# Prologue of a fused cross-attention and expert-FFN kernel: another order of work on five engines

## What is computed

```
x = x + xattn(layernorm(x), ctx)
x = x + ffn(layernorm(x))

xattn:  q, k, v = projections (16 heads of 8);  scores = q k^T / sqrt(8)
        out = softmax(scores v) over the 8 features of a head;  heads @ wo^T + bo
ffn:    t = rmsnorm(x) * norm_w;  2 of 8 experts by softmax(t @ gate^T)
        h1 = t w1^T + 2 (t a1^T) b1^T per expert;  h3 likewise
        act = silu(h1) * h3;  out_e = act w2^T + 2 (act a2^T) b2^T
        out = sum over the two experts, weighted
```

## Time and profile before

| what | us |
|---|---|
| median of 3 runs | 296.5 (296.02 to 297.11) |
| the profiled execution's own time | 295.87 |
| its span | 294.3 |
| PE busy | 286.5 (97%) |
| DVE busy | 220.6 (75%) |
| ACT busy | 183.7 (62%) |
| POOL busy | 180.9 (61%) |

### The profile page before, as it was taken

How to read it: one execution, slowest core, us unless ns; L and a number is a source line. 1 busy time by engine, 2 the same in 40 slices (tenths; PEclk the granted TensorE clock), 3 DMA queues, 4 the chain that set the end, 5 groups by cost and what they waited for, 6 DMA issues and landing times.

```text
span 294.3 us, 4643 instructions
## 1 busy us (share of the span) xinstructions
PE 286.5 (97%) x1531; PEld 240.4 (82%) x1531; DVE 220.6 (75%) x617; ACT 183.7 (62%) x310; POOL 180.9 (61%) x184
## 2 busy tenths in 40 slices
PE   8889999999999999999999999999999999999995
PEld 6767788888888878888888888888888887888884
DVE  3878996986589558993689766894579955795794
ACT  2468967584846866665855948467656648554542
POOL 3377599297960989338890779609882379518400
PEclk9999999999999999999999999999999999999999
DMA  5720020101120020200212011200002001100101
GB/s 144 296 72 1 2 71 0 75 1 49 60 67 4 0 75 36 72 3 0 74 37 71 0 58 51 72 2 1 0 37 74 0 0 38 73 1 0 38 0 36
DMA packets 6666, 12.45 MB, mean 42 GB/s; under 512 B 1266, under 2 KB 2675, under 8 KB 6643
## 3 DMA queue, kind: packets, MB, share of 16 engines
q1 hardware_dynamic: 6208, 11.77, 12.0%
q10 hardware_dynamic: 434, 0.39, 0.4%
HBM read 10.03 MB, written 2.13 MB: 41 GB/s over the span
## 4 chain that ended last, share of the span: by engine, by line
PE 89%; DVE 5%; POOL 2%; issue 1%; ACT 1%; DMA 1%; DVEq 0%; ACTq 0%; POOLq 0%
PE h_ps L647 28%; PE h_ps L633 15%; PE b_ps L698 7%; PE z_ps L698 6%; PE odd_ps L714 6%; PE even_ps L474 4%; PE h_ps L611 3%; PE z_ps L474 3%; PE even_ps L469 2%; PE b_ps L474 2%; PE odd_ps L534 2%; PE b_ps L515 1%; PE z_ps L515 1%; PE odd_ps L469 1%; PE odd_ps L738 1%; DVE stats L1178 1%
## 5 line engine op out<-in xcount | busy, mean ns | idle before, releaser
L1022 ACT ACTIVATE silu<-h_ps 128x512 f32<-128x512 f32 x64 | 37.6, 597 | 37.4 <-PE h_ps L647 35.8
L1703 POOL TENSOR_TENSOR um_lo<-umf,um_hi 128x1024 fp32r<-128x1024 f32 x7 | 16.8, 2407 | 56.4 <-ACT um_hi L1014 56.4
L647 PE MATMUL h_ps<-um_hi,b_hi 128*128 128x512 f32 x128 | 51.3, 401 | 0.0
L647 PE MATMUL h_ps<-um_lo,b_hi 128*128 128x512 f32 x128 | 50.1, 391 | 0.0
L647 PE MATMUL h_ps<-um_hi,b_lo 128*128 128x512 f32 x128 | 49.9, 390 | 0.0
L1361 DVE TENSOR_TENSOR act_second<-silu,h_ps 128x512 f32<-128x512 f32 x32 | 21.8, 681 | 20.0 <-PE h_ps L647 18.1
L1361 DVE TENSOR_TENSOR act_first<-silu,h_ps 128x512 f32<-128x512 f32 x32 | 21.8, 680 | 15.5 <-ACT silu L1022 9.3
L1725 POOL TENSOR_TENSOR scaled<-act_second,ratio 128x512 f32<-128x512 f32 x23 | 29.7, 1294 | 1.8 <-DVE act_second L1361 1.6
L647 PEld LDWEIGHTS h_ps<-um_lo,b_hi 128*128 128x128 f32 x128 | 24.0, 188 | 5.4
L647 PEld LDWEIGHTS h_ps<-um_hi,b_lo 128*128 128x128 f32 x128 | 24.1, 188 | 4.5
L647 PEld LDWEIGHTS h_ps<-um_hi,b_hi 128*128 128x128 f32 x128 | 24.1, 188 | 4.3
(11 more groups left out here) (298 smaller groups left out, 789.9 us busy)
## 6 DMA issues: line engine op xcount, KB each, us to landing
chosen<-choice_dram SPq DMA_DIRECT2D x7, 512.0 KB, 3.6
x_in<-in_x_dram SPq DMA_DIRECT2D x7, 256.0 KB, 3.0
ctx_in<-in_ctx_t_dram SPq DMA_DIRECT2D x7, 256.0 KB, 3.4
out_dram<-y SPq DMA_DIRECT2D x7, 256.0 KB, 2.0
act_second<-in_hidden_w_dram SPq DMA_DIRECT2D x1, 512.0 KB, 4.4
act_second<-in_lora_w_dram SPq DMA_DIRECT2D x1, 512.0 KB, 5.5
v_parts<-in_down_w_dram SPq DMA_DIRECT2D x1, 512.0 KB, 5.5
choice_dram<-choice_t SPq DMA_DIRECT2D x28, 1.0 KB
```

What stands on the lines that cost most here:

```text
L647: mm = nc.tensor.matmul((h1_ps, h3_ps)[s][n % 2][:], b13[w][:, s, c * P:(c + 1) * P], um[k][m][:, s, :], start=False, stop=(i == 2), skip_ ...
L1022: nc.scalar.activation(silu[:, n % SILU_RING, :], h1_ps[n % 2][:], ACT.Silu).then_inc(silu_done.sem, 1)
```

## The change

It changes the order of the lists in the prologue, one bank, and the waits that go with it.

SP: context of block 2 is issued ahead of x of block 2. PE: both halves of block 1's keys and values are made together ahead of the 16 warming matmuls; block 1's k^T v follows right behind block 0's projection and goes to another bank; its output (`attention_out(1)`) moves from behind `first_masks` to between `turn_tok(0, 1)` and `gate(0, 1)`; `first_base(0, 1)`, `first_ratio`, `turn_x(2)`, `turn_heads(1)` and `queries(2)` change places. ACT: all weight casts move up; block 1's queries move between the halves of `tok_turned(0, ...)`; `normal_x(2)` and `x_turned(2)` move down. DVE: `wo_with_bias`, the second half of block 1's keys and values, `mask_ktv(1)` and `first_onehots(1)` move up; `sum_exp(1)` moves ahead of `first_mask_u(1, ...)`. POOL: `low(W13)` moves ahead of `rstd_x(1)` and the heads, `low(B13)` to its old place, `low(WKV)` and `low(W2A2)` ahead of `rstd_x(2)`.

```diff
@@ ktv_bank
-            return pair_b[i] if n == 0 else h1_ps[0] if n < AHEAD else z_ps
+            return pair_b[i] if n == 0 else h3_ps[0] if n < AHEAD else z_ps
@@ SP
+            load_ctx(2)
             load_x(2)
-            load_ctx(2)
@@ keys_times_values
-                if n == 1:
-                    pe.wait_ge(xn_t_done.sem, xn_t_done.of(1))
@@ hidden_bank_free
-                    used = (ktv_done, o_shifted)[n]
+                    used = (xn_t_done, o_shifted)[n]
                     pe.wait_ge(used.sem, used.of(1))
                 elif b == 0:
-                    pe.wait_ge(kv_done.sem, kv_done.of(1, n + 1))
+                    used = (ktv_done, kv_done)[n]
+                    pe.wait_ge(used.sem, used.of(1))
@@ PE
             keys_values_ahead(1, 0)
+            keys_values_ahead(1, 1)
             warm(h1_ps[0], 16)
             turn_heads(0, 0)
             turn_heads(0, 1)
             project(0, 0)
             project(0, 1)
-            keys_values_ahead(1, 1)
+            keys_times_values(1)
             turn_x(1)
...
             queries(1)
             gate(0, 0)
             turn_tok(0, 1)
-            keys_times_values(1)
+            attention_out(1)
             gate(0, 1)
             first_base(1, 1)
             lora_in(0, 0)
             lora_in(0, 1)
             first_masks(0)
             first_masks(1)
-            attention_out(1)
             first_base(0, 0)
+            first_base(0, 1)
+            keys_values(2, 0)
             first_ratio()
-            keys_values(2, 0)
-            first_base(0, 1)
-            turn_x(2)
             first_base(1, 0)
             hidden(0, 0)
+            turn_x(2)
             hidden(0, 1)
+            turn_heads(1)
             queries(2)
-            turn_heads(1)
             keys_values(2, 1)
             project(1)
             hidden(0, 2)
@@ ACT
             queries(0, 0)
             weight_high(A13, attn_w_in, a13, a13_raw)
+            weight_high(W13, hidden_w_in, w13, w13_raw)
             queries(0, 1)
             exp_o(0, 0)
+            weight_high(B13, lora_w_in, b13, b13_raw)
             exp_o(0, 1)
-            weight_high(W13, hidden_w_in, w13, w13_raw)
+            weight_high(W2A2, down_w_in, w2a2, w2a2_raw)
             heads_turned(0, 0)
             heads_turned(0, 1)
             normal_x(1)
-            weight_high(B13, lora_w_in, b13, b13_raw)
+            weight_high(WKV, wkv_in, wkv_split, wkv_sb)
             x_turned(1)
-            weight_high(WKV, wkv_in, wkv_split, wkv_sb)
             tok_turned(0, 0)
+            queries(1)
             tok_turned(0, 1)
             first_spread(0, 0)
             ctx_high(2)
             first_spread(1, 0)
-            queries(1)
             first_spread(0, 1)
             first_spread(1, 1)
             first_masks(0)
             first_masks(1)
             exp_gap(0)
-            normal_x(2)
-            first_ratio()
             first_um_high(0, 0)
             first_um_high(0, 1)
+            first_ratio()
             exp_o(1)
-            x_turned(2)
-            weight_high(W2A2, down_w_in, w2a2, w2a2_raw)
+            normal_x(2)
             first_um_high(1, 0)
             first_um_high(1, 1)
+            x_turned(2)
             silu_step(0, 0)
             heads_turned(1)
@@ DVE
+            wo_with_bias()
             mask_ktv(0, 0)
...
             moments_x(1)
             top_of_o(0, 1)
-            wo_with_bias()
             shift_o(0, 1)
...
             keys_values(1, 0)
+            keys_values(1, 1)
             residual(0, 0)
...
             first_normalise(tok, x1[0], mv2, rstd2, rstd2_done, tok_done, 0)
-            keys_values(1, 1)
+            mask_ktv(1)
             first_normalise(tok, x1[0], mv2, rstd2, rstd2_done, tok_done, 1)
...
             tok_low(0, 1)
             top_logits(0, 1)
+            first_onehots(1)
+            first_gap()
             moments_x(2)
-            first_onehots(1)
-            mask_ktv(1)
-            first_gap()
             first_mask_u(0, 0)
             first_mask_u(0, 1)
             top_of_o(1)
-            first_mask_u(1, 0)
             shift_o(1)
             first_um_low(0)
             first_um_low(1)
+            sum_exp(1)
+            first_mask_u(1, 0)
             first_mask_u(1, 1)
-            sum_exp(1)
             first_diff_low()
@@ POOL
             low(A13, a13, a13_raw)
+            low(W13, w13, w13_raw)
             rstd_x(1)
             norm_heads(0, 0)
             norm_heads(0, 1)
-            low(W13, w13, w13_raw)
+            low(B13, b13, b13_raw)
             first_rstd_x1(0)
             first_rstd_x1(1)
             ctx_low(2)
+            low(WKV, wkv_split, wkv_sb)
+            low(W2A2, w2a2, w2a2_raw)
             rstd_x(2)
-            low(WKV, wkv_split, wkv_sb)
-            low(B13, b13, b13_raw)
             norm_heads(1)
-            low(W2A2, w2a2, w2a2_raw)
             scale_mask(0)
```

## The result

The changed kernel takes 298.51 us (median of 6 runs, 298.13 to 299.81) against 296.6 before (296.02 to 297.11): ratio 1.0068, 95% interval 1.0044 to 1.0093. Forecast were 298.6 and slower. The profiled execution has 298.13 us and a span of 296.6, against 295.87 and 294.3.

A forecast was written before the change was run, and what follows sets the result against it. PE was taken as full from 24 us, with a prologue bound by POOL's heads, then DVE and ACT. +1.18 (heads) and +0.98 (DVE's order, x_turned(2)) made +2.16: 298.6 us against the median of 296.5, range 297.1 to 299.8.

The forecast's parts named there:

- The POOL hold: POOL, ahead of block 1's heads: low(W13) waits for its weights and delays rstd_x(1) from 12.84 to 14.02 us.
- rival 3: POOL: low(W13) takes 3.37 us beside DVE's moments; +3.2 us, 299.7; chance 0.12.
- +1.18: Delay in us of rstd_x(1), passed on to both heads, turned halves, residual, tokens and the first FFN product.
- PE's -1.26: PE before project(1): 1.0 us from block 1's output and 0.26 from the one-hots saved, but spent waiting.
- The -1.0: PE: block 1's output, 1.00 us from 26.93, leaves the stretch in which PE is full.
- The -0.26: PE: the wait inside first_masks(1) for the spread one-hots goes, saving 0.26 us.
- term 2: Stretch from the first FFN product to project(1): DVE's order and x_turned(2) against silu add 0.98 us.
- DVE's order and the table: DVE's sum and reciprocal precede the last masked products; on ACT x_turned(2) then delays table, silu and heads before project(1).
- +0.98: Added us before project(1) from DVE's order and x_turned(2) against silu, with PE's 1.26 spent waiting.
- 1: Rival: only the heads count, block 1's chain on DVE and ACT does not bind; 296.4 to 297.3; chance 0.13.
- 2: Rival: only DVE's order counts, W13 being early enough for heads on time; +0.98, 297.5; chance 0.07.
- 4: Rival: PE's saving carries through and neither chain is late; -1.26, 295.2; chance 0.06.

The follow-up runs named there:

- both terms undone: Changed kernel with a GpSimd list near that of before, silu table behind normal_x(2) and x_turned(2) ahead of the last high parts; ratio to before 1.0032, again 1.0024.
- W13 part early: Kernel before with only W13's cast ahead of queries(0, 1) and its low part ahead of rstd_x(1) on GpSimd; ratio 1.0027.
- sum first: Kernel before with only DVE's order edited, sum_exp(1) ahead of first_mask_u(1, 0) and (1, 1); ratio to before 1.0060.
- the candidates: Two reworkings of the changed kernel with W13's low part behind the heads, 2 warming matmuls and an earlier silu table, placed differently in each; ratios to before 1.0020 and 1.0007.

## Why the prediction was right, point by point

**The POOL hold.** W13's low part at 11.55 (forecast 11.66) for 2.36 (2.35), `rstd_x(1)` at 13.87 (14.02): right, and rival 3 (3.37 long) falls, as the duration was 2.35 or 2.36 in each of the five profiles that had it there. What failed is the constant: "+1.18" was worked out against the one profile of before, which had a quick start. The runs show 0.92 with a quick start and 0.14 with a late one. Three edits were costed at nothing as long as POOL was late (the later queries, `wo_with_bias`, the keys and values ahead of the warming matmuls). The last of them was priced at 0.7 for a POOL on time; it measured 0.47. This is why undoing POOL alone does not give all back: in the quick profile PE turned the heads at 16.05, and without POOL's hold it would have done so at about 15.8 (15.79 in the run with both terms undone), not at 15.3.

**PE's -1.26.** The -1.0 came: the eight matmuls of block 1's output, 0.89 from start to start before, are gone from the full stretch, and what they left was spent waiting, as forecast. The view lists 0.59 for the shifted output (forecast 0.7) and 0.50 for the heads (1.0, PE having come to them later than by my count); for the turned x, where I had 0.5, it lists nothing. The length shows more than this 1.09, since from 12.37 - 0.89 to 13.30 it is 1.82. The rest are delays of at most some 0.25 us each, too short to be listed, behind the one-hots, the shifted output, the turned x and the heads.

The -0.26 for the one-hots did not come. From the first FFN product to the matmul behind the first masks it is 2.84 us before (23.96 to 26.80) and 2.86 after (24.92 to 27.78). That the masks ended at 27.86, as forecast (27.85), is luck: the first product was 0.22 sooner than forecast and took the place of the saving. Nor had the chain of before 0.26 to give there: its two groups of four spread matmuls take 0.24 and 0.40. What kept the one-hots late was DVE, in the changed kernel:

```profile
25.50 0.95 DVE L1308 TENSOR_TENSOR onehot<-rows_sb,top_i 128x16 f32<-128x16 f32 x2
26.48 0.60 DVE L1312 TENSOR_TENSOR onehot<-onehot 128x16 f32<-128x16 f32 x1
```

They took 0.27 and 0.17 in the first half. `moments_x(2)`, which has one SBUF input, had kept them clear of `ctx_low(2)`; moved up, they stand against it and against WKV's low part. A little of this reached the path. The chain of work in the changed kernel runs through them:

```profile
25.50 0.96 DVE onehot L1308 x2
...
26.48 0.04 DVE onehot L1312
```

From the first FFN product to DVE's first masked product it is 3.35 to 3.40 us in the eight profiles with the slow one-hots, and 3.19 to 3.22 in the three that keep the old order (before, W13 part early, sum first; the candidates have an order of their own). So of the 0.93 of term 2, 0.13 to 0.2 probably come from here, a piece that the forecast had not; no run tried it alone.

**DVE's order and the table.** +0.98 forecast, +0.93 and +0.96 measured in the two profiles; 0.77 of it from the order alone, and 0.83 given back by moving the table and `x_turned(2)` alone. The last masked product ends at 34.64 (34.80), the table begins at 35.80 (35.95), `project(1)` at 38.22 (38.52). That the two parts are more than the whole is no contradiction: they are two pieces of one chain, and another wait takes over when either goes.

**Rivals.** 1 falls: the table did bind. 2 falls as a whole, though it describes a late start nearly (0.14 and 0.93 give 1.1). 4 falls; even the best arrangement found only 0.16 us in PE's list.

**The sum.** 2.16 forecast; the spans differ by 2.3 in the first pair, and the medians by 1.9. That the first pair fits so well is luck: the profile of before had a quick start and a timely landing of the chosen experts, that of after neither, so its terms are 0.82 of start, 0.14 of POOL, 0.93 of DVE's order and 0.4 of landing, not 1.18 and 0.98. The second profile of the changed kernel is the fair one to set beside that of before, being quick and timely as well: 0.92 and 0.96 less 0.18 of start give 1.7, and its span is 1.7 longer (296.0 against 294.3). By the traces the change costs 1.9 us with a quick start and 1.1 with a late one. The medians, 1.9 and 1.6 longer in two measurements, lie in that range; how often either start occurs was not measured.

## What to carry to other kernels

An instruction that waits for a large transfer must not stand in a strict list ahead of something on the chain, even if it is "early work": ask what is behind it in its queue. Before work is moved into an engine's idle time, look at what DVE and GpSimd do beside each other there, for both of them, and at how long PE will wait: a wait of 1.5 us cost half the clock here. And compare profiles by a length within the program beside the span, since the moment at which the clock rose moved the start by up to 0.9 us, and one late landing moved the end by over 2.

## What was not expected of the hardware

- The clock can rise to full at 3.91 us in one execution and at 6.88 in another, though PE does the same from 1.0 us on. The float32 matmuls of L496 take 0.63 us ahead of the rise (the first of them 0.74 to 0.79) and 0.38 behind it. The views read 1.00 ahead of the first recorded entry, where nothing is recorded.
- A wait of 1.5 us of PE from 22.6 us on, behind a stretch in which it was busy for 0.47 to 1.00 of each microsecond, was followed by a clock of 0.50 for 6.8 us; waits of 1.2 and 1.3 us between 15.0 and 16.4 us in two other kernels were not.
- GpSimd's small instructions pay as well: the last of `rstd_x(2)`, 0.20 long before, took 0.74 in the changed kernel, beside DVE's low parts of two SBUF tensors that began with it at 30.90.
- The first transfer of the chosen experts, 512 KB from DRAM, landed after 3.29 to 4.43 us in the fourteen profiles. Up to 3.41 it is 257.8 to 258.2 us from `project(1)` to the end; with 3.67 to 3.71, 258.4; with 4.43, 260.4, although PE's listed waits are only 1.1 us of the 2.4.
